# Layer 0 of a graph network: head projections one round later, a new order on VectorE, and dot and cross products of the unmixed vector

## The reference, cut to what matters

```
m1_s, m1_v = _cg_tp(msg_s, msg_v, y0, y1, w...)
val_s = m1_s @ Ws_val
val_v = einsum('ecx,cd->edx', m1_v, Wv_val)          # 64+2*32 channels -> 32, three components
val_v = val_v * sigmoid(val_s @ Wg)[..., None];  val_s = sigmoid(val_s)
m2_s, m2_v = _cg_tp(val_s, val_v, y0, y1, w2_ss, w2_sv, w2_vs, w2_vv0, w2_vv1)
hs = m2_s @ Ws_vlin;  hv = einsum('ecx,cd->edx', m2_v, Wv_vlin)

def _cg_tp(s, v, y0, y1, w...):
    out_s = [w_ss * s * y0,  w_vv0 * dot(v, y1) / sqrt3]
    out_v = [(w_sv * s) y1,  w_vs * v * y0,  w_vv1 * cross(v, y1) / sqrt2]
```

## Time and profile before

| | |
|---|---|
| median of 3 runs | 4853.46 us (4850.1 to 4861.61) |
| profiled execution: first to last instruction (the span) | 3828.1 us |
| what lies around the span, against the median | 1025.4 us |
| the profiled execution's own time outside the span | not given by the profile |
| busy in the span: PE, DVE, ACT, POOL | 89%, 92%, 81%, 67% |
| granted TensorE clock, mean | 0.974 |
| edge pass of layer 0 | about 80 to 2240 us of the span |

### The profile page before, as it was taken

How to read it: one execution, slowest core, us unless ns; L and a number is a source line. 1 busy time by engine, 2 the same in 40 slices (tenths; PEclk the granted TensorE clock), 3 DMA queues, 4 the chain that set the end, 5 groups by cost and what they waited for, 6 DMA issues and landing times. The chain is left out here.

```text
span 3828.1 us, 96308 instructions
## 1 busy us (share of the span) xinstructions
PE 3407.1 (89%) x21340; PEld 2641.0 (69%) x21340; DVE 3541.0 (92%) x12738; ACT 3089.1 (81%) x11217; POOL 2570.9 (67%) x2469
## 2 busy tenths in 40 slices
PE   4899999999999999999999939976999999999997
PEld 3888888888888888888888838864333333333335
DVE  5999999999999999999999978874999999999995
ACT  4888899899989988988899847754787877778774
POOL 1777777777777777777777711111777777777772
PEclk8999999999999999999999979987999999999999
DMA  4333333333333333333333359971333433343333
GB/s 110 89 95 92 92 95 94 92 95 93 95 94 93 95 92 94 93 93 93 94 93 95 93 186 270 274 204 44 92 94 95 95 94 95 95 95 93 95 94 115
DMA packets 299642, 411.02 MB, mean 107 GB/s; under 512 B 98580, under 2 KB 234772, under 8 KB 299316
## 3 DMA queue, kind: packets, MB, share of 16 engines
q0 software_dynamic: 127008, 208.99, 24.2%
q1 hardware_dynamic: 172564, 201.26, 16.3%
HBM read 309.09 MB, written 100.94 MB: 107 GB/s over the span
## 5 line engine op out<-in xcount | busy, mean ns | idle before, releaser
L658 POOL DMA_INDIRECT SC<-dst_tab,idx x784 | 904.5, 1154 | 238.8 <-issue 237.3
L721 POOL DMA_INDIRECT ACC<-hid_tab,idx x784 | 811.4, 1035 | 348.6 <-issue 340.3
L658 POOL DMA_INDIRECT ACC<-src_tab,idx x784 | 758.5, 967 | 313.1 <-issue 164.2
L800 PE MATMUL TR<-ident,M 128*128 128x128 f32 x4704 | 664.4, 277 | 136.9 <-DVE M L1529 135.5
L800 PEld LDWEIGHTS TR<-ident,M 128*128 128x128 f32 x4704 | 520.1, 141 | 229.9 <-DVE M L1529 229.8
L1124 ACT ACTIVATE MT<-TR 128x768 f32<-128x768 f32 x784 | 596.9, 825 | 3.5 <-PE TR L800 3.5
L1113 ACT ACTIVATE ACC<-W,ACC 128x64 f32<-128x64 f32 x2352 | 577.7, 336 | 0.0
L849 PE MATMUL HP<-w_hv,MT 128*128 128x128 f32 x3136 | 520.2, 288 | 0.0
L824 PE MATMUL E<-w_mv,MT 128*128 128x128 f32 x3136 | 476.7, 275 | 0.0
L824 PEld LDWEIGHTS E<-w_mv,MT 128*128 128x128 f32 x3136 | 436.6, 191 | 0.0
L1306 ACT ACTIVATE ACC<-TR,y 128x128 f32<-128x128 f32 (+1 forms) x1568 | 417.2, 551 | 1.3 <-PE TR L982 1.2
(11 more groups left out here) (278 smaller groups left out, 7662.5 us busy)
## 6 DMA issues: line engine op xcount, KB each, us to landing
h_tab<-ACC SPq DMA_DIRECT2D x392, 160.0 KB
SC<-h_tab SPq DMA_DIRECT2D x50, 640.0 KB, 4.8
TAB<-h_tab SPq DMA_DIRECT2D x48, 640.0 KB, 5.2
ACC<-in_e64T SPq DMA_DIRECT2D x98, 256.0 KB
ACC<-src_tab,idx POOLq DMA_INDIRECT x784
SC<-dst_tab,idx POOLq DMA_INDIRECT x784
ACC<-hid_tab,idx POOLq DMA_INDIRECT x784, 3.4
agg_tab<-ACC POOLq DMA_DIRECT2D x49, 240.0 KB, 4.0
```

The costliest lines, as they stand in the source:

```text
L658: pool.indirect_dma_start(gat[:, v.slot8, g, :], None, table.ap(), bass.IndirectOffsetOnAxis(ap=idx[:, v.sslot, c + g:c + g + 1], axis=0))\
L721: pool.indirect_dma_start(gat1[:, v.slot8, g, :], None, hid_tab.ap(), bass.IndirectOffsetOnAxis(ap=idx[:, v.sslot, c:c + 1], axis=0))\
L800: ins = nc.tensor.transpose(to[:, b * G + g, :], Mt[:, g, lo:lo + w], ident[:, :])
```

## The change

- PE: `hm` works on chunk t-3 instead of t-2 and is issued between `t2` and `t1`, not after `factors0`. MT2 gets a second buffer (`MT2b`), so c2 waits for the hm of two chunks ago. The widths of the three projections per g are 192, 128 and 96 columns instead of 64, 128, 128, all into one accumulating region of HP of 192 columns.
- The mixed vector is no longer formed. V2 now holds gate times the four 32-column parts of E1 (three components and the scalar part). DVE forms four products with y1, y2, y3 and |y1|^2 (`fD2`), and one reduction adds them to the dot product; the cross product of the scalar part with y1 vanishes; the scalar part goes to PE as further channels, with w_hs0 and w_hv0 laid out anew. `svy` and `vals` are gone.
- |y1|^2 is computed once, ahead of the loop, into a fifth plane of `y_all`, which is now a tile of its own with the component as the outer index.
- DVE's order: `messages`, `summed`, `products0`, `crossed0`, `scaled`, `mixed_dots`, `head_products` (chunk t-3), `mixed_crosses`, sums, `others0`, `head_values`, the rest.
- ACT: line 1152 copies 128 instead of 96 columns; `scalars0` and SP's store work on chunk t-3. The tail is 3 rounds instead of 2.
- One more memset on POOL (w_hs0) ahead of the weight loads.

```diff
@@ PE
-            def turn(Mt, to, sem_done):
+            def turn(Mt, blocks, to, sem_done):
...
                 for g in range(G):
-                    nc.tensor.matmul(HP[:, S * g:S * (g + 1)], MT2[:, 0, g, :], w_hs0[:, :], start=True, stop=True)
-                    for b in range(2):
-                        ins = nc.tensor.matmul(HP[:, P + P * g:P + P * (g + 1)], MT2[:, 1 + b, g, :], w_hv0[:, b, :],
-                                               start=(b == 0), stop=(b == 1))
+                    o = HP[:, 192 * g:192 * (g + 1)]
+                    nc.tensor.matmul(o, MT2s[v.par][:, 1, g, :], w_hv0[:, 0, :], start=True, stop=False)
+                    nc.tensor.matmul(o[:, 0:P], MT2s[v.par][:, 2, g, :], w_hv0[:, 1, 0:P], start=False, stop=False)
+                    ins = nc.tensor.matmul(o[:, 96:192], MT2s[v.par][:, 0, g, :], w_hs0[:, :], start=False, stop=True)
...
                 e1(t + -1, total)
                 t2(t + -2, total)
+                hm(t + -3, total)
                 t1(t, total)
                 factors0(t + 2, total)
-                hm(t + -2, total)
-            loop_steps(pe, Q, NS, False, 2, 2, stage0)
+            loop_steps(pe, Q, NS, False, 2, 3, stage0)
@@ ACT
-                if v.past(1):
-                    act.wait_ge(LA[freed], v.num)
+                if v.past(back):
+                    act.wait_ge(LA[freed], v.num + 1 - back)
...
-                    ins = nc.scalar.activation(M2[:, v.par, g, C + P:2 * P], V2[:, g, :], ACT.Copy, scale=y_at(v, g, 0))
+                    ins = nc.scalar.activation(M2[:, v.par, g, P:2 * P], V2[:, g, :], ACT.Copy, scale=y_at(v, g, 0))
...
-                copies(t + -2, total, "t2", TR2, MT2, "c2", "h")
-                copies(t, total, "t1", TR1, MT, "c1", "e1")
+                copies(t + -2, total, "t2", TR2, MT2s[(t + -2).par], "c2", "h", 2)
+                copies(t, total, "t1", TR1, MT, "c1", "e1", 1)
                 weigh2(t + -1, total)
                 weigh0(t + 2, total, 0)
-                scalars0(t + -2, total)
+                scalars0(t + -3, total)
@@ DVE, before the loop
+            y_sq = mf[:, 800:800 + NC]
+            ch.step(TT(y_all[:, 4, :], y_all[:, 1, :], y_all[:, 1, :], ALU.mult))
+            for k in (2, 3):
+                ch.step(TT(y_sq, y_all[:, k, :], y_all[:, k, :], ALU.mult))
+                ch.step(TT(y_all[:, 4, :], y_all[:, 4, :], y_sq, ALU.add))
@@ DVE
-                TT(k3(V2[:, :, :]), ax(gate[:, v.par, 0, 0:1], (C, G), (0, 3), (1, C)), vals[:, :, :, :], ALU.mult)\
-                    .then_inc(LA["vg"], 1)
+                TT(ax(V2[:, 0, 0:1], (P, G), (C, 4), (1, C)), ax(gate[:, v.par, 0, 0:1], (C, G), (0, 4), (1, C)),
+                   ax(E1[:, 1, 0:1], (P, G), (C, 4), (1, C)), ALU.mult).then_inc(LA["vg"], 1)
...
+                return ch.count(TT(fD2[:, :, :, :], vec(0, (C, 4), (1, C)), y_of(v, 1, (NC, 4), (0, C)), ALU.mult))
...
-                    TT(M2[:, v.par, :, C:2 * C], M2[:, v.par, :, 0:C], M2[:, v.par, :, C:2 * C], ALU.add)
+                    if v.past(2):
+                        dve.wait_ge(LA["t2"], v.num - 1)
+                    nc.vector.tensor_reduce(M2[:, v.par, :, 0:C], ax(fD2[:, 0, 0, 0:1], (P, G), (1, C), (C, 4)), AX.X, ALU.add)
...
                 gated(t + -1, total)
                 added = messages(t + 1, total)
-                ups = gated_up(t + -1, total)
-                done = summed(t + -1, total, ups)
+                summed(t + -1, total)
                 parts = products0(t + 1, total, added)
-                scaled(t + -1, total, done)
                 crossed0(t + 1, total, parts)
-                mixes = mixed(t + -1, total)
-                mixed_sums(t + -1, total, mixes)
-                up = head_products(t + -2, total)
+                scaled(t + -1, total)
+                dots = mixed_dots(t + -1, total)
+                up = head_products(t + -3, total)
+                crosses2 = mixed_crosses(t + -1, total)
+                sum_of_dots0(t + 1, total, parts)
+                mixed_dot_sums(t + -1, total, dots)
+                mixed_cross_sums(t + -1, total, crosses2)
                 crosses = others0(t + 1, total, parts)
-                head_values(t + -2, total, up)
+                head_values(t + -3, total, up)
                 rest_of_s0(t + 1, total, parts)
                 rest_of_v0(t + 1, total, parts, crosses)
@@ POOL and SP
-            sp.wait_ge(s_zero, 13)
+            sp.wait_ge(s_zero, 14)
...
-                store(t + -2, total)
+                store(t + -3, total)
```

More of the change, by code:

```diff
@@ L260, in program @@
         MT2 = sb("MT2", [P, 4, G, P])
+        MT2s = (MT2, sb("MT2b", [P, 3, G, P]))
         tr_n = MT2[:, :, :, :].rearrange("p (a b) g e -> p a (b g) e", a=2)
@@ L422, in _ @@
                 load(ws_val_t[:, r], a["Ws_val_T"][:, q])
-                load(w_hs0[r, :], a["Ws_vlin"][q, :])
-                load(w2s[r, :], rows(a["w2_ss"] if q.start == 0 else a["w2_vv0"]))
+            load(w2s[0:C, :], rows(a["w2_vv0"]))
+            load(w2s[C:S, :], rows(a["w2_sv"])[0:C, :])
+            load(w2s[S:P, :], rows(a["w2_ss"]))
             for k in range(3):
@@ L427, in _ @@
                 load(w2v[C * k:C * (k + 1), 1:2], rows(a["w2_vv1"]))
-            for b in range(2):
-                load(w2v[96:128, b:b + 1], rows(a["w2_sv"])[C * b:C * (b + 1), :])
+            load(w2v[96:128, 0:1], rows(a["w2_vs"]))
+            load(w2v[96:128, 1:2], rows(a["w2_sv"])[C:S, :])
             load(wg[:, :], a["Wg"])
@@ L466, in _ @@
             load(w_mv0[0:64, 0, 96:128], a["Wv_val"][0:64, :])
-            for b in range(2):
-                load(w_hv0[96:128, b, 96:128], a["Wv_vlin"][C * b:C * (b + 1), :])
+            load(w_hv0[96:128, 0, 96:128], a["Wv_vlin"][64:96, :])
+            load(w_hv0[96:128, 1, 96:128], a["Wv_vlin"][C:S, :])
+            load(w_hs0[0:C, C:C + S], a["Ws_vlin"][S:96, :])
+            load(w_hs0[S:P, C:C + S], a["Ws_vlin"][0:S, :])
+            load(w_hs0[C:S, 0:C], a["Wv_vlin"][0:C, :])
             n_const[0] = n
-            sp.dma_start(y_all, a["y_line"]).then_inc(s_y, 16)
+            sp.dma_start(y_all[:, 0:4, :], a["y_line"]).then_inc(s_y, 16)
             for i in range(5):
@@ L809, in t1 @@
                     pe.wait_ge(LA["c1"], v.num)
-                turn(M[:, v.par], TR1, LA["t1"])
+                turn(M[:, v.par], B0, TR1, LA["t1"])
             def e1(v, total):
@@ L1115, in weigh0, with copies @@
                     ins.then_inc(LA["ws"], 1)
-            def copies(v, total, turned, tr, dst, sem_done, freed):
+            def copies(v, total, turned, tr, dst, sem_done, freed, back):
                 if not inside(v, total):
@@ L1555, in summed, with scaled @@
                                                  ax(la[:, 0, 0:1], (LG, G * H), (1, LG)), AX.X, ALU.add))
-                ch.wait(up)
-                return ch.count(TT(vals[:, :, :, :], ax(E1[:, 1, 0:1], (P, G), (C, 3), (1, C)), svy[:, :, :, :], ALU.add))
-            def scaled(v, total, summed):
+            def scaled(v, total):
                 if not inside(v, total):
@@ L1584, in mixed @@
[L1584 to L1591 removed]
+                    return ax(V2[:, 0, C * k:C * k + 1], (P, G), *dims)
@@ new lines, in mixed_dots, with mixed_crosses, vec @@
+                return ch.count(TT(fD2[:, :, :, :], vec(0, (C, 4), (1, C)), y_of(v, 1, (NC, 4), (0, C)), ALU.mult))
+            def mixed_crosses(v, total):
+                if not inside(v, total):
+                    return
+                def vec(k, *dims):
+                    return ax(V2[:, 0, C * k:C * k + 1], (P, G), *dims)
+                TT(fX2[:, :, 0:2, 0, :], vec(0, (C, 2), (1, C)), y_of(v, 2, (NC, 2), (0, C)), ALU.mult)
+                TT(fX2[:, :, 0:2, 1, :], vec(1, (C, 2), (1, C)), y_of(v, 1, (NC, 2), (0, C)), ALU.mult)
+                return ch.count(TT(fX2[:, :, 2], vec(2, (-2 * C, 2), (1, C)), y_of(v, 1, (2 * NC, 2), (0, C)), ALU.mult))
```

80 lines of the change are left out of this document (35 added, 45 removed).

## The result

The changed kernel takes 5063.97 us (median of 4 runs, 5056.67 to 5068.54), the kernel before 4857.53 in the same comparison: ratio 1.0435, interval 1.0404 to 1.0466. I had forecast slower, but 4890 and at most 4925 us. It is slower, and by 206 us, not 37.

The account below looks back on a forecast made before the run. VectorE and GpSimd were taken to bound the kernel at nearly 5.46 us a round; new chains would make it 5.55, 392 rounds giving +35, plus 1 drain, rounded to +37: 4890 us, range 4800 to 4925.

Parts of the forecast that it names:

- Sum: Total: 392 rounds times (5.55 - 5.46) plus drain, +37 us; span 3865, plus 1025.4 us left outside the span, 4890 us.
- VectorE's part: VectorE's steps in layer 0's edge loop: -0.22 us a round, so its own pace 5.24 us at most.
- nothing dearer than the product: Bound on VectorE's new reduction over 256 inputs: no more than a product's 0.33 us (+0.20), and 0.02 more.
- Chain B: From t1 through ScalarE's round, its read hs of bank HP, to the end of hm: 5.55 us, deciding the round.
- Chain A: From t1 to next t1 through copy c1, e1, t2 and hm, all serial: 5.50 us a round.
- GpSimd's part: Gathers in the edge loop: shorter beside fewer VectorE products from SBUF, 5.1 to 5.2 us a round, bounds 5.00 to 5.46.
- The time around the span: The runs' median 4853.5 us lies 1025.4 us above the profiled span; this rest was left unchanged.
- Rival 1: Faster: chains shorter than summed, the round falls to VectorE's and GpSimd's 5.2 us, -102 us, 4751 us; chance 0.20.
- Rival 2: Nothing to see: hm's block takes 1.43 us or GpSimd's stretch stays, 4844 to 4863 us; chance 0.20.
- Once-only terms: Setup and drain outside the steady rounds: squares of y 0, one memset under 1 us and hidden, drain +1 us.

Follow-up runs that it names:

- VectorE was eased: Changed kernel with scaled ahead of crossed0 and the 256-input reduction made of two adds: 3899.0 us at clock 1.00, 5113.73 and 5125.55 with the clock halved.
- hs was early: Changed kernel with both VectorE edits, and ScalarE's read of HP moved ahead of the copy of t1's result: 3840.06 us at clock 1.00, 5108.74 with the clock halved.
- lean version: Changed kernel with the projections' order of before, scaled ahead of crossed0 and two adds for the reduction: 3778.01 us at clock 1.00 (ratio 0.9892).
- the order alone: Kernel before with only hm one round later and ahead of t1, second MT2 buffer and steps following it: 5091.97 us clock halved, 3820.89 at 1.00.
- version without those chains: Changed kernel with hm, head_products, hs and store back in the places of before, new VectorE steps and wide projections kept: 3909.17 us at clock 1.00.

## Why the prediction was wrong

**Direction right, size and first cause wrong.** Two steps failed. The first is the end of "Sum": the 1025.4 us "outside the span" that I left alone. They lay inside the runs, in rounds at a halved clock, so rows at clock 1.00 could not price the change there. It cost +206 us, not +37, and the order, for which I had 0.09 us a round, is alone enough for 0.61 there (7.444 to 8.058).

The second is "VectorE's part", and it is the one at clock 1.00, where my rows belong and the change cost +89 us: I gave VectorE's round as 5.24 at most, it is 5.665. Three terms were mis-sized, all start to start. The reduction was put at the product's 0.33; it is 0.516 (+0.18). `mixed_dots` was put at 0.33 behind `scaled`; it is 0.551, because `crossed0` no longer stands between them (+0.22). And from the reduction of the logits (L1562) to the next start 0.30 pass, where `vals` used to follow after 0.21 (+0.09); the next one now reads the message sum with two fewer instructions between, so probably a dependency again, which no run tests. Before, the medians of VectorE's distances from start to start sum to 5.39; less 0.22 and plus 0.49 comes 5.66. The bound "nothing dearer than the product" rested on durations, 372 against 350 ns; the duration of an instruction did not tell its pitch. At the new size the duration is 599 ns, so it would have been a warning.

**Chain B: right, 0.08 short, and not first.** Forecast 5.55, read 5.63; 5.62 once VectorE was eased, and gone once hs was early. With VectorE eased it cost +71 us by itself, so it would have given the direction too. Of the 0.08 the block has 0.05: its first 192-wide pair takes 0.40 us (1007.93 to 1008.33), where I had 0.33. That is so only where the block starts behind its wait for hs. With hs early the first pair takes 0.33 us, the second 0.35 as here, and the block 1.52, so 1.54 was a fair price. The Trainium skill, in "TensorE: Matmul & The Clock Gate", section Back-to-back issue gap, describes weight loads pipelined with the matmuls, which would favour the lower 1.43; the rows show 1.52 to 1.59, so the measurement decides against it.

**Chain A: right**, 5.50 forecast, 5.48 measured where it was left alone.

**GpSimd's part: wrong.** The SC gathers got longer, from 1157 to 1283 ns, the ACC ones shorter, from 964 to 945. All the same busy plus "issue" is the full 1600 us, with VectorE at 5.665 and waiting for nothing. So a GpSimd that is never free is no proof that it sets the pace: here its gathers stretch to the round. It is the same in the lean version, with gathers of 1.02 us on average, a round of 5.31 us and VectorE waiting for nobody. Only in the profiled execution of 3897.57 us (1.12 us, round 5.69) did VectorE wait for them in most rounds. Three of a round's four gathers take 0.95 us, and the one long gather runs beside the last products of VectorE's round (L1536, L1542, L1543), three in a row from SBUF:

```profile
1006.25 0.95 POOL L663 DMA_INDIRECT ACC<-src_tab,idx  x1 [0.30 <-issue]
1007.50 1.62 POOL L663 DMA_INDIRECT SC<-dst_tab,idx  x1 [0.30 <-issue]
```

By the rule of the Trainium skill in "GPSIMD Engine Reference", section 1 Specifications, contention with VectorE's instructions of two SBUF inputs is to be expected. The trace agrees only in part: the gather at 1006.25 runs beside such instructions too (L1608 at 1006.40 and the two after it) and takes 0.95 us all the same. What makes one gather of four long is open.

**The time around the span: wrong.** It was the clock. 392 x (8.023 - 7.444) = +227 us lie in the edge pass where it is halved, and 12 us come back outside it (the two spans differ by 214 us), against a kernel before of another chip. All seven kernels with the order took 7.86 to 8.19 us a round there, whatever they took at 1.00 (5.44 to 5.67 for those measured); the one without took 7.44. That the order is enough is shown. How much the new steps add there is open: the order alone gave +250, the changed kernel +206, on different chips. Why easing VectorE made kernels slower there is open too, and so is what the wide projections cost there.

**Rivals.** Rival 1 asked for chains shorter than summed; they were not. Its engines' sums were wrong too: the version without those chains still took 3909, and only with VectorE's two edits 3778. Rival 2's block of 1.43 us did not come either. Once-only terms were as forecast: the first message sum starts at 86.4 us, before at 86.9, and the rest is the same within 1 us.

## What to carry to other kernels

Price a VectorE step by the distance to the next start in a row of that very operation and size, and look at what stood between a producer and its reader: an independent instruction between them was free here, and moving it away cost 0.22 us. Ask of each reordering what cover it takes from a copy that TensorE waits for: at clock 1.00 the order alone cost nothing, and with the clock halved 250 us. And check the span against the run's time before explaining a difference: 1000 us here were a clock.

## What was not expected of the hardware

The same program took 3821 to 3828 us on two chips and 4834 to 4858 on others. In the steady stretch the granted clock was 1.00 throughout on the former and 0.90 on average on the latter, where the run of before had 98 drops to half in 2400 us (from 300 to 2700). They go with a far greater loss than the mean says: the round grew by 37% (5.443 to 7.444) at a mean clock 10% lower. In the drop shown a result of TensorE came over 4 us late before the lower clock was on record. What makes the clock drop on one chip and not on another no run here tells.
